# Four equal weight buffers in a fused graph-attention, linear-attention and mixture-of-experts layer

## The reference, cut to what matters

```python
xn = _layernorm(x)
x = x + gnn(xn, edges, wq, wk, wv, wiq, wik, wiv, wo) + mix(xn, Wq, Wkv, Wo, ln_gamma, ln_beta)
...
def gnn(x, ...):                       # N = 96, H = 16 heads of 64
    q, k, v = x @ wq.T + bq, x @ wk.T + bk, x @ wv.T + bv
    q2, k2, v2 = q @ wiq.T + biq, k @ wik.T + bik, v @ wiv.T + biv
    attn = softmax(q2 @ k2.T / 8 + mask)
    return (attn @ v2) @ wo.T + bo
def mix(h, ...):                       # sequence length 1: the sum over j has one term
    q, k, v = h @ Wq, h @ Wkv[:, :D], h @ Wkv[:, D:]
    ...                                # products of relu features, a ratio per head
    return layer_norm(h + attn_vec @ Wo)
...
xn = _layernorm(x)
scores = sigmoid(xn @ gate_w.T)        # top 2 of 8 experts for each token
h = relu(bf16((xn * score) @ w_up[e].T)) ** 2
routed = bf16(h @ w_down[e].T)         # summed over the two experts of a token
out = x + routed + relu(xn @ shared_w_up.T) ** 2 @ shared_w_down.T
```

## Time and profile before

| | us |
|---|---|
| median of 3 runs (lowest, highest) | 370.77 (370.04, 371.83) |
| the profiled execution's own time | 369.9 |
| its span (first to last instruction) | 368.2 |
| TensorE matmul busy | 301.4 (82%) |
| VectorE, ScalarE, GpSimd busy | 107.9, 39.6, 30.7 |

### The profile page before, as it was taken

The page is one execution under the profiler, slowest core; times in us unless marked ns, Lnnn a source line. Parts: engine busy times, 40 slices in busy tenths (PEclk is TensorE's granted clock), DMA queues, the critical chain, the costliest instruction groups (busy, mean ns, idle before and its releaser), DMA issues.

```text
span 368.2 us, 6488 instructions
## 1 busy us (share of the span) xinstructions
PE 301.4 (82%) x2808; PEld 242.4 (66%) x2808; DVE 107.9 (29%) x249; ACT 39.6 (11%) x81; POOL 30.7 (8%) x56
## 2 busy tenths in 40 slices
PE   5999999999999999999699999999546456454442
PEld 4999999996443344333699999988536355453432
DVE  6609407300164296007433201023110011011001
ACT  1400000000030011100302110012101001001101
POOL 0400000000001000200002214013211000000000
PEclk9999999999999999999679999999955655556768
DMA  8999999999999998999999999999999999999994
GB/s 311 428 421 425 400 312 371 360 303 385 324 355 386 345 352 283 303 325 301 296 330 331 214 215 218 215 216 216 213 218 215 215 216 214 216 213 217 216 213 106
DMA packets 11699, 105.07 MB, mean 285 GB/s; under 512 B 1313, under 2 KB 1849, under 8 KB 3997
## 3 DMA queue, kind: packets, MB, share of 16 engines
q0 software_dynamic: 6912, 46.14, 60.2%
q1 hardware_dynamic: 4576, 58.46, 38.9%
q10 hardware_dynamic: 188, 0.14, 0.1%
HBM read 150.48 MB, written 0.39 MB: 410 GB/s over the span
## 4 chain that ended last, share of the span: by engine, by line
PE 73%; DMA 13%; another core or an unknown queue 9%; DVE 2%; issue 1%; ACT 1%; POOL 0%; POOLq 0%; ACTq 0%
PE bank L829 22%; PE bank L820 20%; DMA stage<-in_expert_up 13%; PE bank L987 7%; PE bank L970 7%; PE bank L939 6%; PE bank L1016 5%; PE bank L791 1%; PE bank L806 1%; PE bank L930 1%; PE bank L1000 0%; PE bank L874 0%; PE bank L904 0%; PE bank L889 0%
## 5 line engine op out<-in xcount | busy, mean ns | idle before, releaser
L820 PE MATMUL bank<-xnt,ring 128*128 128x96 f32 x384 | 45.4, 283 | 0.6 <-ACT xnt L354 0.6
L820 PEld LDWEIGHTS bank<-xnt,ring 128*128 128x128 f32 x384 | 45.0, 199 | 1.0 <-ACT xnt L354 0.9
L970 PE MATMUL bank<-xe,stage 128*128 128x96 bf16 x528 | 30.9, 231 | 14.1 <-DMA stage<-in_expert_up 13.2
L829 PE MATMUL bank<-ring,xnt 128*96 128x512 f32 x96 | 41.6, 593 | 0.0
L829 PE MATMUL bank<-ring,stage 128*96 128x512 f32 x96 | 41.5, 592 | 0.0
L987 PE MATMUL bank<-hbuf,stage 128*128 128x96 bf16 x528 | 29.4, 225 | 14.0 <-DMA stage<-in_expert_down 12.3
L970 PEld LDWEIGHTS bank<-xe,stage 128*128 128x128 bf16 x528 | 29.2, 113 | 15.5 <-issue 12.5
L987 PEld LDWEIGHTS bank<-hbuf,stage 128*128 128x128 bf16 x528 | 27.8, 109 | 15.5 <-issue 8.8
L829 PEld LDWEIGHTS bank<-ring,xnt 128*96 128x96 f32 x96 | 15.5, 163 | 24.6 <-issue 24.5
L829 PEld LDWEIGHTS bank<-ring,stage 128*96 128x96 f32 x96 | 15.5, 163 | 24.5 <-issue 24.5
L820 PE MATMUL bank<-stage,ring 128*128 128x96 f32 x256 | 28.8, 275 | 0.0
(11 more groups left out here) (148 smaller groups left out, 202.1 us busy)
## 6 DMA issues: line engine op xcount, KB each, us to landing
stage<-in_expert_down POOLq DMA_DIRECT2D x12, 1056.0 KB, 32.8
stage<-in_expert_up POOLq DMA_DIRECT2D x12, 1024.0 KB, 23.6
stage<-in_expert_up POOLq DMA_DIRECT2D x6, 768.0 KB, 30.0
stage<-in_expert_down POOLq DMA_DIRECT2D x6, 704.0 KB, 28.7
ring<-in_expert_down POOLq DMA_DIRECT2D x4, 1056.0 KB, 64.8
ring<-in_mat_wq SPq DMA_DIRECT2D x2, 2048.0 KB, 10.8
ring<-in_mat_wk SPq DMA_DIRECT2D x2, 2048.0 KB, 20.3
ring<-in_mat_wv SPq DMA_DIRECT2D x2, 2048.0 KB, 21.6
```

The lines of the kernel that those rows point to most:

```text
L820: ins = mm(bank[BANKS[m] + h][:, o * N:(o + 1) * N], slots[c % SLOTS][:, k, o * P:(o + 1) * P], tiles(src)[:, k, :], start=(k == 0), stop= ...
L829: ins = mm(bank[BANKS[m] + h][0:N, :], tiles(src)[:, k, :], slots[c % SLOTS][:, k, :], start=(k == 0), stop=(k == KT - 1))
L970: ins = mm(bank[4 + j][:, (t - t0) * N:(t - t0 + 1) * N], up[:, t, k, :], tiles(xe[:])[:, k, :], start=(k == 0), stop=(k == KT - 1))
```

## The change

The 176 KB a partition of weight memory are cut into four equal buffers instead of two and a double one.

- `stage[0]`, `stage[1]` and `stage[2]` hold experts; expert e goes to buffer e mod 3. The arena is now `stage[2]`, so expert 1 needs no part of it, and expert 2 goes in it.
- The ring is the fourth buffer: five slots of 8 KB a partition (`PIECE`), with gamma behind them. A half is loaded as two pieces of 1 MB by two DMAs; TensorE waits for each piece, and counts them (`front_done` for the first of a half, `half_done` for the second). Piece p waits until piece p - 5 has been used. The matrices lie in memory as four contiguous pieces each.
- The shared up weights follow into the same ring in six DMAs (five of 1 MB and one of 0.5 MB), each as a slot comes free, the last after `pre_ready`. The shared down weights (three DMAs) go over the shared up weights, and are asked for when TensorE has used those: the first after shared tiles 4 to 6, the other two after the last tile.
- GpSimd asks for part k of experts 0 to 2 when `FIRST_PARTS[k]` pieces have been used: parts 0 and 1 at the start (part 0 when piece 1 has landed), then two parts for about seven pieces. The parts of expert 2 wait besides for the arena. Experts 3 to 7 follow part by part as the expert three before is used, written out without a loop.
- `beta`, `w_all` and `xe` share one tensor, `out_t` is `acc_t`, and `mvec_t` is `xnt`. No instruction is added on DVE or ACT.

```diff
-SLOT = KT * HALF
+BUF = TT * D
+PIECE = KT * HALF // 2
+PIECES = 2
 SLOTS = 5
...
+FIRST_PARTS = [0, 1, 5, 8, 12, 15, 19, 22, 26, 29, 33, 36, 38, 41, 43, 43, 44, 44]
...
-        ring = sb("ring", [P, 2 * TT * UNIT], F32)
-        stage = [sb(f"stage{b}", [P, TT * UNIT], F32)[:, :] for b in range(2)]
...
-        arena = stage[1]
+        stage = [sb(f"stage{b}", [P, BUF], F32)[:, :] for b in range(3)]
+        ring = sb("ring", [P, BUF], F32)
+        slots = [ring[:, s * PIECE:(s + 1) * PIECE] for s in range(SLOTS)]
...
+        arena = stage[2]
...
+        def piece_landed(eng, piece):
+            eng.wait_ge(slot_landed[slot_of(piece)], 16 * (piece // SLOTS + 1))
+
+        def pieces_used(eng, n):
+
+            if n % PIECES:
+                eng.wait_ge(front_done, n // PIECES + 1)
+            else:
+                eng.wait_ge(half_done, n // PIECES)
...
             for c, (m, h) in enumerate(STEPS):
-                if c >= SLOTS:
-                    sp.wait_ge(half_done, c - SLOTS + 1)
-                dst = ring[:, (c % SLOTS) * SLOT:(c % SLOTS + 1) * SLOT]
-                sp.dma_start(dst, mats[m][h]).then_inc(slot_landed[c % SLOTS], 16)
...
+                for i in range(PIECES):
+                    piece = c * PIECES + i
+                    if piece >= SLOTS:
+                        pieces_used(sp, piece - SLOTS + 1)
+                    slot = slot_of(piece)
+                    sp.dma_start(slots[slot], mats[m][h * PIECES + i]).then_inc(slot_landed[slot], 16)
+
+            for j in range(SLOTS + 1):
+                if j < SLOTS:
+                    pieces_used(sp, len(STEPS) * PIECES - SLOTS + j + 1)
+                else:
                     sp.wait_ge(pre_ready, 1)
...
+                f0, f1 = j * PIECE, min((j + 1) * PIECE, BUF)
+                sp.dma_start(ring[:, f0:f1], shared_up[:, f0:f1]).then_inc(sh_up_landed[j], 16)
+            for j, (o0, o1) in enumerate(OUT_TILES):
+
+                sp.wait_ge(up_done, up_before(2) - (j == 0))
+                sp.dma_start(ring[:, o0 * DUNIT:o1 * DUNIT], shared_down[:, o0 * DUNIT:o1 * DUNIT])\
+                  .then_inc(sh_dn_landed[j], 16)
...
+            piece_landed(pool, 1)
+            load(0, 0, 0)
             pool.wait_ge(bias_v_landed, 16)
...
+            for part in range(1, 2 * 2 * PARTS):
+                pieces_used(pool, FIRST_PARTS[part])
...
+                load(part // 6, part % 6 // PARTS, part % PARTS)
             pool.wait_ge(pv_psum, 2)
             pool.wait_ge(mvec_t_psum, 2)
...
+            for part in range(2 * 2 * PARTS, 3 * 2 * PARTS):
+                pieces_used(pool, FIRST_PARTS[part])
+                load(part // 6, part % 6 // PARTS, part % PARTS)
+
+            for e in range(3, EXPERTS):
+                for j in range(PARTS):
+                    pool.wait_ge(up_done, up_before(e - 3) + j + 1)
+                    load(e, 0, j)
+                for j in range(PARTS):
+                    pool.wait_ge(down_done, down_before(e - 3) + j + 1)
+                    load(e, 1, j)
```

More of the change, by code:

```diff
@@ L72, in gps_layer @@
         bank = [ctx.enter_context(nc.psum_tensor(f"bank{i}", [P, 512], F32)) for i in range(8)]
[L77 to L90 removed]
+        stage = [sb(f"stage{b}", [P, BUF], F32)[:, :] for b in range(3)]
+        ring = sb("ring", [P, BUF], F32)
+        slots = [ring[:, s * PIECE:(s + 1) * PIECE] for s in range(SLOTS)]
+        gamma = ring[:, SLOTS * PIECE:SLOTS * PIECE + D]
+        sh_up_t = ring[:, :].rearrange("p (t k j) -> p t k j", t=TT, k=KT)
+        arena = stage[2]
         def sh_dn(o, t):
[L93 to L98 removed]
+            return ring[:, o * DUNIT + t * P:o * DUNIT + (t + 1) * P]
         def take(at, n):
@@ L177, in gps_layer @@
         slot_landed = [sem(f"slot_landed{s}") for s in range(SLOTS)]
-        shared_landed = [sem(f"shared_landed{j}") for j in range(2 * PARTS)]
+        sh_up_landed = [sem(f"sh_up_landed{j}") for j in range(SLOTS + 1)]
+        sh_dn_landed = [sem(f"sh_dn_landed{j}") for j in range(PARTS)]
         stage_landed = [[sem(f"stage_landed{b}_{j}") for j in range(2 * PARTS)] for b in range(3)]
@@ L282, in _, with load @@
         def _(pool):
+            def load(e, m, j):
+                b = e % 3
+                f0, f1 = [(t * UNIT, o * DUNIT)[m] for t, o in zip(TILES[j], OUT_TILES[j])]
+                place = stage[b].rearrange("p (m n) -> p m n", m=2)[:, m, :].bitcast(BF16)
+                pool.dma_start(place[:, f0:f1], (expert_up, expert_down)[m][e, :, f0:f1])\
+                    .then_inc(stage_landed[b][PARTS * m + j], 16)
+            piece_landed(pool, 1)
+            load(0, 0, 0)
             pool.wait_ge(bias_v_landed, 16)
@@ L287, in _ @@
             nc.gpsimd.partition_broadcast(beta, beta[0:1, :]).then_inc(spread, 1)
[L289 to L295, removed]
@@ L298, in _ @@
[L298 to L304, removed]
+            for part in range(1, 2 * 2 * PARTS):
+                pieces_used(pool, FIRST_PARTS[part])
+                if part == 9:
+                    pool.wait_ge(bias_o_landed, 16)
+                    nc.gpsimd.partition_broadcast(bias_o_b, bias_o_b[0:1, :]).then_inc(spread, 1)
+                load(part // 6, part % 6 // PARTS, part % PARTS)
@@ L816, in out_transposed @@
                 c = AT[m, h]
[L817 to L823, removed]
+                for i in range(PIECES):
+                    piece = c * PIECES + i
+                    w = slots[slot_of(piece)].rearrange("p (k n) -> p k n", k=KT)
+                    piece_landed(pe, piece)
+                    for o in range(HT // PIECES):
+                        at = i * (HT // PIECES) + o
+                        for k in range(KT):
+                            ins = mm(bank[BANKS[m] + h][:, at * N:(at + 1) * N],
+                                     w[:, k, o * P:(o + 1) * P], tiles(src)[:, k, :],
+                                     start=(k == 0), stop=(k == KT - 1))
+                    ins.then_inc(front_done if i == 0 else half_done, 1)
             def out_rows(m, h, src):
                 c = AT[m, h]
[L827 to L831, removed]
+                for i in range(PIECES):
+                    piece = c * PIECES + i
+                    w = slots[slot_of(piece)].rearrange("p (k n) -> p k n", n=HALF)
+                    piece_landed(pe, piece)
+                    for kk in range(KT // PIECES):
+                        k = i * (KT // PIECES) + kk
+                        ins = mm(bank[BANKS[m] + h][0:N, :], tiles(src)[:, k, :], w[:, kk, :],
+                                 start=(k == 0), stop=(k == KT - 1))
+                    ins.then_inc(front_done if i == 0 else half_done, 1)
             for h in range(2):
@@ L970, in expert @@
                             ins = mm(bank[4 + j][:, (t - t0) * N:(t - t0 + 1) * N], up[:, t, k, :],
-                                     tiles(xe[:])[:, k, :], start=(k == 0), stop=(k == KT - 1))
+                                     tiles(xe)[:, k, :], start=(k == 0), stop=(k == KT - 1))
                     ins.then_inc(up_done, 1)
@@ L1010, in _ @@
                 pe.wait_ge(out_taken, PARTS + j + 1)
-                for part in ((0, 1), (2,), ())[j]:
-                    pe.wait_ge(shared_landed[PARTS + part], 16)
+                pe.wait_ge(sh_dn_landed[j], 16)
                 for o in range(o0, o1):
@@ L1021, in _ @@
                     e = i * 3 + (2 + n)
-                    expert(e, n, i + (n < 2), (added, e * PARTS) if n == 0 else (out_taken, e * PARTS - PARTS))
+                    expert(e, (2, 0, 1)[n], i + (n > 0), (added, e * PARTS) if n == 0 else (out_taken, e * PARTS - PARTS))
 def kernel(**inputs):
```

43 lines of the change are left out of this document (19 added, 24 removed).

## The result

The changed kernel takes 365.38 us (365.01 to 366.04, 4 runs) against 370.63 us of the kernel before beside it (370.04 to 371.83, 4 runs). The ratio is 0.9856, 95% interval 0.9828 to 0.9885: 1.4% faster, 5.3 us where 3.3 were forecast, inside the range. The same kernel run again later took 365.09 us (ratio 0.9848, 0.9828 to 0.9869).

A forecast was written before the change was run, and what follows sets the result against it. DMA transfers were taken to bound the kernel, ending with the last landing plus 4.0 us. Closing the gap (-4.6) and 25 more DMAs (+1.3) sum to -3.3: 370.8 to 367.5 us, range 363.5 to 373.

The forecast's parts named there:

- DMA work bounds it, the gap goes: Whole kernel: time ends with the last transfer plus 4.0 us; the DMA gap from 129.4 to 147.5 us closes.
- The gap's size, -4.6: Loads-only window 129.4 to 147.5 us: rate 317 instead of 425 GB/s, 4.6 us lost, all to be won.
- Mixing, 0 with 3.8 at worst: Casts and loads side by side from 8 to 225 us: loss taken as 0, bounds +3.8 and -1.9 us.
- rival A: The gap closes, but mixing casts and loads takes 3.8 us back: 371 us, no difference; chance 0.22.
- 25 more DMAs, +1.3: Smaller loads of matrices 22 to 44 and shared up weights: 0.05 us for each added DMA, +1.3 us.
- Rival B: Small transfers cost 0.3 us a DMA, 7.6 us for 25: 373.8 us, slower; chance 0.09.
- The 50 us: Cost of the 25 added DMAs, unhidden, by the Trainium skill's fixed 2.0 us for each on GpSimd's path.
- Its bound from the casts, 0.3 us at most: Added DMAs: upper price for each beside its bytes, read from cast landings, 7.6 us for 25.
- 9 to 11 us in hand: At TensorE's starts of pieces 12, 24 and 36: 9 to 11 us of asked-for DMA work always in hand.
- TensorE late by 1 to 4 us, at no cost: End of TensorE's front: 1 to 4 us late, near 177 instead of 174.4 us, costing nothing at the end.
- Shared down weights, 2 us of wait, worth 0: Before the shared down matmuls: TensorE stands still some 2 us; later experts wait for DMA anyway, so 0.
- Rival C: TensorE's front: casts starve loads of shorter rows, pauses halve its clock, DMA runs dry: 376 us; chance 0.09.

The follow-up runs named there:

- split loads: Kernel before, each 2 MB half loaded by two, four or eight DMAs instead of one: 370.47, 371.84 and 375.19 us.
- asks_4_later: Kernel after, every part after the first asked for four pieces later, none after piece 44: 367.38 us.
- asks_10_later: Kernel after, parts 1 to 17 asked for ten pieces later, none after piece 44: 375.80 us.
- asks_as_before: Kernel after, parts of experts 0 and 1 asked for at about the pieces of the kernel before, expert 2 at 44: 381.72 us.
- one_expert_early: Kernel after, parts 1 to 5 of expert 0 asked for at 1 to 5 pieces instead of 1, 5, 8, 12 and 15: 374.18 us.
- asks_2_earlier: Kernel after, parts 2 to 13 asked for two pieces earlier, the last four one or two pieces earlier: 366.30 us.
- after_again: Kernel after, unchanged, run again later beside other runs: 365.09 us, ratio to before 0.9848.
- the last split: Kernel before, each 2 MB half loaded by eight DMAs of 2 KB rows instead of one: 375.19 us against 370.50.

## Why the prediction was right, point by point

- **DMA work bounds it, the gap goes.** Right. The gap near 140 us closed, the last landing moved by the whole gain, and 6 us of TensorE's lateness cost nothing.
- **The gap's size, -4.6: the term that was mis-sized.** I read it from one window and took the 1.9 us lost from 42 to 129 us for a property of mixing, with no change. Counted as for the kernel after: when the shared up weights are asked for, at 144.65 us, 22 halves (108.5), one expert (27.0) and the start (2.4) have been asked for, 137.9. So 6.7 us were forced, wherever they showed. Less 1.3 for smaller rows this gives 5.4; measured are 5.3. That more work before 144.65 us is nearly free is shown by the split loads.
- **Mixing, 0 with 3.8 at worst (rival A).** The worst case didn't happen: from 3 to 156.4 us the balance closes within 0.6 us with casts under way nearly all the time.
- **25 more DMAs, +1.3.** Right in size: 420 instead of 425 GB/s on 51.9 MB is 1.4 us. (With 427, the 16 KB rate in the same window as the 420, it would be 2.0.) Rival B's 0.3 us a DMA is excluded by the rates: one DMA more for a half costs 0.06 us. The 50 us that the prediction set beside it took a figure for GpSimd's path; the 25 added DMAs are SyncE's. Its bound from the casts, 0.3 us at most, is the mean of 0.03 and 0.58.
- **9 to 11 us in hand.** Wrong: the step looked at three places, and counted the work just after an ask. Just before the ask at 32.75 us it is 1.7 us. That it had no effect on the sum is luck: the margin could as well have been below 0, and four pieces later cost 2.0 us.
- **TensorE late by 1 to 4 us, at no cost.** It was 6.2 us, outside the range named for the front's end. At no cost is right, with 5.6 us of cover left.
- **Shared down weights, 2 us of wait, worth 0.** 4.1 us, worth 0; the first part was waited for, since it was asked for at 218.8 us and not near 212, and needed 14.7 us.
- **Rival C.** Its split didn't come about in the kernel after: the first cast beside 8 KB pieces needed 12.8 us from issue to landing, against 15.2 beside 16 KB rows. In the kernel before itself, with only the rows halved, it is 13.0. Its clock loss appears when casts are bunched.

The count against the runs, in us, all from the work asked for just before the named ask:

| kernel | ask at | work asked for | forced | measured over after | last landing later by |
|---|---|---|---|---|---|
| before | 144.65 | 137.9 | 6.7, less 1.3 for rows | 5.3 | 5.2 |
| asks_4_later | 32.60 | 29.6 | 3.0 | 2.0 | 2.5 |
| asks_10_later | 70.04 | 59.3 | 10.7 | 10.7 | 10.8 |
| asks_as_before | 145.09 | 129.1 | 16.0 | 16.3 | 15.5 |
| one_expert_early | 96.98 | 86.6 | 10.4 | 8.8 | 9.2 |
| asks_2_earlier | 208.37 | 206.8 | 1.6 | 1.2 | 1.5 |

Asks_2_earlier and asks_10_later are taken over after_again, the others over the first runs of after. The last column is from the profiled executions alone. Forced idle time ought to be a lower bound, and in one_expert_early and asks_4_later less was lost than was forced: the count is good to about 1.6 us, no better, and why is open. The numbers in the table were all made with the trace at hand. On record before the run, by the same count, stood asks_10_later (10.1 forced, 375.5 us: met), asks_as_before (18.7, 384 us: 2 us too many) and asks_2_earlier (nothing forced: 1.2 us slower, outside its 0.7). The slack of 6.65 us in the kernel before was on record ahead of the last split (4 to 6 us slower forecast, 4.7 measured). Asks_4_later was forecast by the work in hand after an ask, and one_expert_early by the cover before expert 3 alone; both missed.

## What to carry to other kernels

Where transfers bound a kernel, don't size a gap by the window in which it shows. Take each ask that waits for something, and subtract from its time all the work asked for *before* it: the largest difference is the idle time that the order of asks forces, and work placed ahead of it is free up to that amount, as long as it doesn't make the ask itself later. A smaller ring with well-timed asks beats a larger one here, but the same buffers with the old asks lose 11 us; the list of asks is the change, and it has under 2 us to spare toward later asks and under 6 toward a later TensorE.

## What the runs showed of the hardware

Loads of SyncE's queue alone, 2 MB each, moved 425, 420, 409 and 386 GB/s with rows of 16, 8, 4 and 2 KB. Each halving of the rows costs more than the one before: 1.2, 2.6 and 5.6% (the first 1.6% with the 427 of the same window). The first cast of 1 MB (as written) beside such loads, in the same kernel with the same amount of loads in the ring, landed 15.2, 13.0, 11.6 and 11.1 us after its issue beside rows of 16, 8, 4 and 2 KB; casts behind one another take 4.87 us each. So the shorter rows did give the casts more of the engines, though far from twice as much for each halving.
